# Edge counts of a graph kernel: one routing register a step, and the low one-hots of the late steps made on GpSimd

## The chip, the cores and the metric

The kernel runs on one core of a Trainium2 chip. Its time is the device time in microseconds of one execution. The engines are TensorE (PE for its matmuls, PEld for its weight loads, PEldq or PEq for its sequencer), VectorE (DVE), ScalarE (ACT), GpSimd (POOL) and SyncE (SP), which issues transfers.

## The reference, cut to what matters

A graph of 3125 nodes and 53125 directed edges, sorted by destination, passes through four networks of 128 features (a graph convolution, a two-head attention layer behind a second convolution, a gated network of five layers, an eight-head attention network). The first layer computes

```python
xw = x @ W
deg = jax.ops.segment_sum(ones, dst, num_segments=N)
dinv = jnp.where(deg > 0, jax.lax.rsqrt(deg), 0.0)
norm = dinv[src] * dinv[dst]
msg = xw[src] * norm[:, None]
h = jax.ops.segment_sum(msg, dst, num_segments=N) + b
```

The kernel does most of the sums over edges as dense products. For that it first counts, for each pair of nodes, the edges between them, and keeps the counts as a matrix in DRAM (`adj`). The change lies in that count and in the start of the layer behind it.

## The kernel before, in words

`adjacency_tables` (0 to 36.5 us) reads the edges and prepares, for each of 611 steps, two values for each of 128 edges: `keyt`, which says where among 400 columns the edge counts, and `lowt`, the low seven bits of its source. A step is one tile of 128 edges in one window of 16 destination nodes; there are 196 windows.

`adjacency_counts` runs the steps, each engine through its own list and held to the others by semaphores:

- VectorE makes for step j a one-hot of 400 columns, `count_hot` (line 886, a ring of 8), and every eighth step a block `count_low` (line 876, a ring of 3) with the low one-hots of the next eight steps: 1024 columns, the eight steps interleaved.
- TensorE multiplies the two (line 958, `made`) and adds the product into the PSUM bank of the step's window, one of four. Which bank and which window is data: every fourth step its sequencer loads eight registers from `route_r` (line 923), two a step, moves them (line 924), and before each matmul waits for the step's one-hot (`hots`) and, in an instruction of its own (line 957), for the bank to be free (`freed`, compared with a register).
- ScalarE copies each finished window to `count_stage` (line 975) and clears its bank (line 978). SyncE stores the window to `adj` (line 987).
- Between the steps, by tables of step numbers, TensorE and VectorE also do other work: 20 products that fold two weight matrices of the gated network (lines 938 and 900, from step 40 every 12), five rounds that count the degrees (lines 842 and 846, from step 100), and from step 342 the product x @ W, scaled into `own` (lines 952, 954, 909, 912).
- GpSimd fetches rows for the degrees (line 809), makes `h`, the normalised and rectified x (lines 813 and 816, 70.5 to 94.4 us), stores the folded weights (line 819) and the norms (lines 821 and 823), and casts `own` to the high part of `gcn_parts` (line 827).

After a barrier of all engines `gcn_first` multiplies `gcn_parts`, a high and a low part for each 128 nodes, with the counts. SyncE loads the columns of `adj` in eight groups. VectorE makes the low parts (line 1073), adds the identity to the loaded columns (line 1051, `add_own`) and casts them into `gcn_stream` (line 1061, `widen`); TensorE's matmuls are at line 1138.

## Time and profile before

| | us |
|---|---|
| median of 3 runs | 3405.78 (3403.04 to 3406.25) |
| the profiled execution, its own time | 3405.62 |
| its span, first to last instruction | 3403.8 |
| tables, to the barrier | 36.5 |
| counts, first matmul of a step to the last | 38.3 to 330.5 |
| first matmul of `gcn_first` | 340.3 |

Over the span TensorE is busy 82%, VectorE 52%, ScalarE 40%, GpSimd 28%. These are averages over stages with different limits; for this change only the first 350 us are read. A row of the waits says who waited, and what came last before it could go on; "issue" is time in which an engine's unit had nothing handed to it and no semaphore explains it. Shares of a sequencer are not counted as busy time, so its instructions are read by their durations and by the gaps they leave.

### The profile page before, as it was taken

To read this page: it belongs to the slowest core of one execution; us is meant where nothing else is said; L and a number is where in the kernel's file an instruction comes from. 1 tells how busy PE (TensorE), PEld (TensorE's weight loads), DVE (VectorE), ACT (ScalarE), POOL (GpSimd) and SP (SyncE) were. 2 spreads that over 40 slices of the span, in tenths; PEclk is the share of its full clock that TensorE was granted. 3 is DMA by queue.
4 is the path that set the end of the run, shared out by engine and by line. 5 is a ranking of instruction groups with operands and counts; after the bars stand their busy time and mean duration, and the time that the engine had idled before them with its cause. 6 is when DMAs were issued, how large, how long until landed. Compare 5 with 4: busy or idle time off the path is not lost. (4 is left out here: it accounts for less than half of the span.)

```text
span 3403.8 us, 41036 instructions
## 1 busy us (share of the span) xinstructions
PE 2807.8 (82%) x13998; PEld 2155.1 (63%) x13998; DVE 1760.0 (52%) x4016; ACT 1368.7 (40%) x2596; POOL 961.7 (28%) x779
## 2 busy tenths in 40 slices
PE   5776977899998699999999999999844445446998
PEld 3333875577776578787877787877533334445775
DVE  7987765999977452111122112111534543356994
ACT  3565034699997221111111112111323333342896
POOL 6100043000000453232322231321177777750000
PEclk9977979899999799999999999999855555555999
DMA  4232633101100432121212121310242221113100
GB/s 135 100 101 88 263 130 155 39 40 40 44 1 1 192 150 97 58 92 68 87 63 90 65 92 57 116 70 1 74 141 47 46 46 38 29 21 126 78 35 20
DMA packets 79695, 266.66 MB, mean 78 GB/s; under 512 B 21129, under 2 KB 53344, under 8 KB 70176
## 3 DMA queue, kind: packets, MB, share of 16 engines
q1 hardware_dynamic: 62520, 236.50, 18.6%
q0 software_dynamic: 16976, 27.54, 3.7%
q8 instruction: 121, 1.98, 0.2%
q14 instruction: 78, 0.64, 0.1%
HBM read 232.80 MB, written 31.18 MB: 78 GB/s over the span
## 5 line engine op out<-in xcount | busy, mean ns | idle before, releaser
L2799 PE MATMUL psum<-gate_stream,parts 128*128 128x384 f32 (+1 forms) x3600 | 667.9, 344 | 16.9 <-POOL gate_stream L2872 12.5
L2799 PEld LDWEIGHTS psum<-gate_stream,parts 128*128 128x128 f32 x3600 | 631.5, 189 | 33.8 <-issue 14.4
L2872 POOL CAST gate_stream<-gate_adj 128x1920 fp32r<-128x1920 f16 (+1 forms) x200 | 371.1, 1863 | 851.3 <-PE psum L2799 828.2
L2153 PE MATMUL psum<-gat_h,gat_pair 128*128 128x129 f32 (+1 forms) x3750 | 571.1, 291 | 8.6 <-DVE gat_pair L1957 7.7
L2153 PEld LDWEIGHTS psum<-gat_h,gat_pair 128*128 128x128 f32 (+1 forms) x3750 | 461.5, 191 | 123.4 <-issue 77.7
L1485 POOL DMA_INDIRECT edge_rows<-edge_table,src_idx x440 | 431.7, 981 | 180.7 <-issue 133.7
L2890 DVE SCALAR_TENSOR_TENSOR gate_work<-psum,bhh,gate_work 128x384 f32<-128x384 f32 (+1 forms) x80 | 50.0, 626 | 793.7 <-PE psum L2762 763.1
L1957 DVE SCALAR_TENSOR_TENSOR gat_pair<-gat_above,gat_adj 128x512 f32<-128x512 f32 (+3 forms) x525 | 326.6, 622 | 86.8 <-PE psum L2153 56.7
L2066 ACT ACTIVATE gat_above<-psum,gat_as 128x512 f32<-128x512 f32 (+3 forms) x525 | 329.7, 628 | 41.4 <-PE psum L2141 39.9
L2057 ACT ACTIVATE psum<-gat_ad_rows,gat_as 128x512 f32<-128x512 f32 (+3 forms) x525 | 334.9, 638 | 16.9
L1912 DVE SCALAR_TENSOR_TENSOR gat_acc<-gat_adj,gat_q,gat_acc 128x512 f32<-128x512 f16 (+3 forms) x497 | 328.4, 677 | 0.0
L2816 ACT COPY x<-psum 128x384 f32<-128x384 f32 (+1 forms) x72 | 31.9, 488 | 545.5 <-PE psum L2799 545.5
L1722 PE MATMUL psum<-edge_rows,edge_hot 128*128 128x81 f32 x826 | 179.6, 419 | 86.0 <-DVE edge_rows L1621 86.0
L1722 PEld LDWEIGHTS psum<-edge_rows,edge_hot 128*128 128x128 f32 x826 | 177.2, 332 | 87.6 <-issue 87.2
L958 PE MATMUL psum<-count_hot,count_low 128*128 128x400 f16 x611 | 172.9, 412 | 69.8 <-DVE count_hot L886 47.2
L2141 PE MATMUL psum<-gat_r_rows,gat_pick 6*128 6x512 bf16 (+7 forms) x525 | 189.1, 361 | 0.9 <-ACT gat_r_rows L2075 0.9
L958 PEld LDWEIGHTS psum<-count_hot,count_low 128*128 128x128 f16 x611 | 88.6, 146 | 155.1 <-issue 122.3
L886 DVE TENSOR_SCALAR count_hot<-iota_hot,keyt 128x400 f16<-128x400 f16 x611 | 175.5, 339 | 16.3 <-PE psum L958 13.3
L2844 ACT ACTIVATE gate_work<-psum,brz 128x384 f32<-128x384 f32 (+1 forms) x80 | 47.1, 588 | 331.7 <-PE psum L2775 331.7
L2383 POOL MEMSET parts<- 128x512 f32 x1 | 0.5, 526 | 547.3 <-POOLq L2283 547.3
L975 ACT CAST count_stage<-psum 128x400 f16<-128x400 f32 x196 | 96.8, 494 | 126.2 <-PE psum L958 124.6
L1649 ACT ACTIVATE edge_hot<-iota,edge_minus 128x128 f32<-128x128 f32 x413 | 121.3, 391 | 6.2 <-PEq L2458 6.2
(486 smaller groups left out, 3700.8 us busy)
## 6 DMA issues: line engine op xcount, KB each, us to landing
gate_adj<-adj SPq DMA_DIRECT2D x35, 2400.0 KB, 8.1
gat_adj<-adj SPq DMA_DIRECT2D x8, 3200.0 KB, 11.3
adj<-count_stage SPq DMA_DIRECT2D x196, 100.0 KB, 1.6
gcn_adj<-adj SPq DMA_DIRECT2D x8, 2400.0 KB, 8.2
edge_place<-row_scratch SPq DMA_DIRECT2D x40, 352.0 KB, 3.8
gate_adj<-adj SPq DMA_DIRECT2D x5, 2800.0 KB, 9.1
gcn_adj<-adj SPq DMA_DIRECT2D x4, 3200.0 KB, 10.0
edge_rows<-edge_table,src_idx POOLq DMA_INDIRECT x440
```

The source lines that it names most:

```text
L886: e.tensor_scalar(hot[:, j % HRING, :], iota_hot[:], keyt[:, j:j + 1], None, ALU.is_equal).then_inc(hots, 1)
L958: e.matmul(flat[:, bass.ds(at[j % 4], ROW)], low[:, j // LS % LRING, :, j % LS], hot[:, j % HRING, :], start=False, stop=False, skip_group ...
L1485: e.indirect_dma_start(out=rows[:, c % 2, s, 0:ROWS], out_offset=None, in_=table, in_offset=bass.IndirectOffsetOnAxis(ap=self.src_idx[:, k ...
L1722: mm = e.matmul(flat[:, bass.ds(to[k % 4], SUMS)], hot_of(c)[:, s, :], rows[:, c % 2, s, :], start=False, stop=False, skip_group_check=True)
L1912: e.scalar_tensor_tensor(on, of, q[:, hi, h:h + 1], on, ALU.min, ALU.max).then_inc(most, 1)
L1957: e.scalar_tensor_tensor(on(pair, g % 2), on(above, g % 3), 1e30, cols[:, u % ring, 0:width(u) // W, hi * W:(hi + 1) * W], ALU.min, ALU.mu ...
L2057: e.activation(ps[:, 4 + g % 3, 0:up - lo], ad_rows[:, h, lo:up], ACT.Relu, bias=as8[:, hi, h:h + 1], scale=1.0 - NEG).then_inc(relus, 1)
L2066: e.activation(above[:, g % 3, 0:width(u)], ps[:, 4 + g % 3, 0:width(u)], ACT.Exp, bias=as2[:, hi, h:h + 1]).then_inc(exps, 1)
L2141: e.matmul(ps[:, 4 + g % 3, 0:width(u)], pick[:, h, :], r2_rows[:, u % 2, 0:width(u)], start=False, stop=False, skip_group_check=True).the ...
L2153: mm = e.matmul(ps[0:p, b, a:a + D + 1], pair[:, g % 2, i * P:i * P + p], h1[:, hi, h, :], start=hi == 0 and i % 3 == 0, stop=hi == NT - 1 ...
L2799: mm = e.matmul(ps[:, f, 0:hi - lo], parts[:, t, m, f, :], stream[:, (NGG * i + t // GG) % GR, 0:windows(i), t % GG * W:(t % GG + 1) * W], ...
L2872: e.tensor_copy(stream[:, n % GR, 0:windows(i), :], cols[:, i % 2, 0:windows(i), g * GW:(g + 1) * GW]).then_inc(widened, 1)
```

## The change

1. `route_r` holds one value a step, the window plus 2, instead of two. TensorE's sequencer loads four registers every fourth step and works the bank out of each with a register instruction. The bank of a window moves on by one (lines of ScalarE likewise). The wait for a free bank comes at even steps only, for the bank of the step behind.
2. From step 240 (`LATE` = 30 blocks of 8) VectorE makes no more low one-hots. GpSimd makes them, one comparison of 128 columns a step, from a float32 copy of `lowt` (`lowf`, two more copies on ScalarE in the tables) against the same ring of three blocks, now one step behind the other in it. It starts a block when the steps of the block three before are done, and signals each block (`lower`).
3. GpSimd's other work in the counts is put between its blocks; the low part of `gcn_parts` is now made there too, by a subtraction behind each cast.
4. The first two groups of columns of `adj` are loaded within the counts, and the identity is added to them behind the last steps.
5. Buffers share memory to make room: `near` lies in `gcn_parts`, the weights to be folded in `own`, some tables in `folded`, `h` and `norms`.

```diff
@@ adjacency_tables, vector
-                e.tensor_scalar(win_i[:], win_r[:], 1.0, None, ALU.add).then_inc(made, 1)
+                e.tensor_scalar(route_r[:, 0:BP], win_r[:], 2.0, None, ALU.add).then_inc(made, 1)
...
-                e.tensor_scalar(win_i[:], win_i[:], WR - 1, 9, ALU.bitwise_and, ALU.logical_shift_left).then_inc(made, 1)
-                e.tensor_scalar(route_r[:, 0:BP, 1], win_r[:], 2.0, None, ALU.add)
...
-                e.tensor_copy(route_r[:, 0:BP, 0], win_i[:])
@@ adjacency_tables, scalar
                 e.copy(lowt[:, per * BK:BP], ps[:, 5, 0:BP - per * BK])
+                e.copy(lowf[:, 0:per * BK], ps[:, 4, 0:per * BK])
+                e.copy(lowf[:, per * BK:BP], ps[:, 5, 0:BP - per * BK])
@@ adjacency_counts
+        late = low[:].rearrange("p r q j -> p (r q j)").rearrange("p (r j q) -> p r j q", r=LRING, j=LS)
...
-        near = self.sb("node_near", [P, NT, SE], F32, st)
+        near = parts[:].rearrange("p t m w -> p t (m w)").bitcast(F32)
...
+        own_at = {BSTEPS - 1: (0, 0), BSTEPS - 2: (1, 0), BSTEPS - 3: (1, 1), BSTEPS - 4: (1, 2)}
@@ adjacency_counts, gpsimd
+                def split(n):
+
                     at = slice(group(n)[0], group(n)[-1] + 1)
                     e.wait_ge(hw_taken, n + 2)
-                    e.tensor_copy(parts[:, at, 0, :], own[:, at, :])
+                    e.tensor_copy(parts[:, at, 0, :], own[:, at, :]).then_inc(shaped, 1)
+                    e.wait_ge(shaped, n // 2 + 3)
+                    e.tensor_tensor(parts[:, at, 1, :], own[:, at, :], parts[:, at, 0, :], ALU.subtract)
+
+                for l in range(3):
+                    lay(l)
+                for m in range(LATE, -(-BSTEPS // LS)):
+                    e.wait_ge(made, LS * (m - 2))
+                    for i in range(LS):
+                        inst = e.tensor_scalar(late[:, m % LRING, i, :], self.iota[:], lowf[:, m * LS + i:m * LS + i + 1], None, ALU.is_equal)
+                    inst.then_inc(lower, 1)
+                    if m == 31:
+                        lay(3)
+                    if m == 37:
+                        lay(4)
...
+                    if m >= 48 and m % 4 == 0 and m <= 72:
+                        split((m - 46) // 2)
@@ adjacency_counts, vector
-                    if j % LS == 4 and j + 4 < BSTEPS:
+                    if j % LS == 4 and j // LS + 1 < LATE:
                         lows(j // LS + 1)
...
+                    if j in own_at:
+                        c, i = own_at[j]
+                        t, p = tiles[c][i]
+                        e.wait_ge(loaded[c], 16)
+                        on = cols[:, c, 8 * i:8 * i + p // W, t * W:(t + 1) * W]
+                        e.tensor_tensor(on, on, ident_h[:, 0:p].rearrange("p (w n) -> p w n", n=W), ALU.add)
@@ adjacency_counts, tensor
-                regs = [e.alloc_register(self.name("route_reg")) for _ in range(8)]
...
-                    if j % 4 == 0:
-                        e.load(regs, route[0:1, 2 * j:2 * j + 8])
-                        at = [e.snap(r, min_val=0, max_val=(WR - 1) * 512) for r in regs[0::2]]
-                        need = [e.snap(r, min_val=1, max_val=NW) for r in regs[1::2]]
+                    if j % RL == 0:
+                        regs = [e.alloc_register(self.name("route_reg")) for _ in range(RL)]
+                        e.load(regs, route_r[0:1, j:j + RL])
+                        need = [e.snap(r, donate=True, min_val=1, max_val=NW) for r in regs]
+                        at = [(n & (WR - 1)) * 512 for n in need]
...
+                    if j % LS == 0 and j >= LS * LATE:
+                        e.wait_ge(lower, j // LS - LATE + 1)
                     e.wait_ge(hots, j + 1)
-                    e.wait_ge(freed, need[j % 4])
+                    if j % 2 == 0:
+                        e.wait_ge(freed, need[min(j + 1, BSTEPS - 1) % RL])
@@ adjacency_counts, sync
+                    for c, (lo, hi) in enumerate(spans[:2]):
+                        if w == hi // W + SRING:
+                            for s in range(SRING):
+                                e.wait_ge(stored[s], 16 * (hi // W // SRING))
+                            e.dma_start(cols[:, c, 0:(hi - lo) // W, :], self.adj[:, lo // W:hi // W, :]).then_inc(loaded[c], 16)
@@ gcn_first, vector
-                for n in range(NT // grp):
-                    at = slice(n * grp, (n + 1) * grp)
-                    e.tensor_tensor(parts[:, at, 1, :], own[:, at, :], parts[:, at, 0, :], ALU.subtract).then_inc(far, 1)
...
-                add_own(1)
+                for g in range(NGG):
+                    widen(0, g)
```

TensorE's instructions in the count loop, one group of four steps, before ("ISA" is a register instruction of the sequencer, `freed` and `hots` the waits):

```order
L923 TENSOR_LOAD route_r
L924 ISA
L958 ISA [waits counts_freed,counts_hots]
L958 MATMUL psum<-count_hot,count_low 128x400
L958 ISA [waits counts_freed,counts_hots]
L958 MATMUL psum<-count_hot,count_low 128x400
L958 ISA [waits counts_freed,counts_hots]
L958 MATMUL psum<-count_hot,count_low 128x400
L958 ISA [waits counts_freed,counts_hots]
L958 MATMUL psum<-count_hot,count_low 128x400
```

and now:

```order
L954 TENSOR_LOAD route_r
L992 REGISTER_ALU [waits counts_freed,counts_hots]
L992 ISA
L992 MATMUL psum<-count_hot,count_low 128x400
L992 REGISTER_ALU [waits counts_hots]
L992 ISA
L992 MATMUL psum<-count_hot,count_low 128x400
L992 REGISTER_ALU [waits counts_freed,counts_hots]
L992 ISA
L992 MATMUL psum<-count_hot,count_low 128x400
L992 REGISTER_ALU [waits counts_hots]
L992 ISA
```

The load stands for four registers, the move behind it (line 924) is gone, each step has one register instruction more, and the wait for `freed` stands at every second step.

VectorE around step 240, before (the block of low one-hots, the one-hots, and what is strewn among them):

```order
L876 TENSOR_TENSOR count_low<-iota_low,lowt 128x1024 [waits counts_made]
L886 TENSOR_SCALAR count_hot<-iota_hot,keyt 128x400
L886 TENSOR_SCALAR count_hot<-iota_hot,keyt 128x400 [waits counts_made] x2
L900 COPY folded<-psum 128x384 [waits fold_laid1,fold_made]
L886 TENSOR_SCALAR count_hot<-iota_hot,keyt 128x400 [waits counts_made] x2
L852 MEMSET node_after 128x1 [waits degree_ended]
L853 COPY node_after<-node_until 128x24
L886 TENSOR_SCALAR count_hot<-iota_hot,keyt 128x400 [waits counts_made] x3
L876 TENSOR_TENSOR count_low<-iota_low,lowt 128x1024 [waits counts_made]
L886 TENSOR_SCALAR count_hot<-iota_hot,keyt 128x400
L886 TENSOR_SCALAR count_hot<-iota_hot,keyt 128x400 [waits counts_made] x6
L900 COPY folded<-psum 128x384 [waits fold_laid0,fold_made]
```

and now:

```order
L900 TENSOR_TENSOR count_low<-iota_low,lowt 128x1024 [waits counts_made]
L911 TENSOR_SCALAR count_hot<-iota_hot,keyt 128x400
L911 TENSOR_SCALAR count_hot<-iota_hot,keyt 128x400 [waits counts_made] x2
L931 COPY folded<-psum 128x384 [waits fold_laid1,fold_made]
L911 TENSOR_SCALAR count_hot<-iota_hot,keyt 128x400 [waits counts_made] x2
L876 MEMSET node_after 128x1 [waits degree_ended]
L877 COPY node_after<-node_until 128x24
L911 TENSOR_SCALAR count_hot<-iota_hot,keyt 128x400 [waits counts_made] x10
L931 COPY folded<-psum 128x384 [waits fold_laid0,fold_made]
L911 TENSOR_SCALAR count_hot<-iota_hot,keyt 128x400 [waits counts_made] x12
```

The block at the head of each list is the one of steps 232 to 239; before, the next block (steps 240 to 247) follows after eight one-hots; now there is none behind it.

GpSimd at the same place, before, from the stores of folded rows to the end of the counts:

```order
L819 DMA folded_rows<-folded 128x1536 [waits fold_kept] x5
L821 DMA norm_rows<-norm_t 25x128 [waits first_taken]
L823 DMA norms<-norm_rows 128x3200 [waits first_norm_kept]
L827 CAST gcn_parts<-own 128x4x128 [waits first_taken] x6
L827 CAST gcn_parts<-own 128x128 [waits first_taken]
L805 UNCONDITIONAL_BRANCH [waits fold_laid1,fold_laid0,first_norm_in]
```

and now, from the first comparisons on (the block of steps 240 to 247), and around the first cast of `own`:

```order
L838 TENSOR_SCALAR count_low<-iota,ht_15 128x128 [waits counts_made]
L838 TENSOR_SCALAR count_low<-iota,ht_15 128x128 x7
L838 TENSOR_SCALAR count_low<-iota,ht_15 128x128 [waits counts_made]
L838 TENSOR_SCALAR count_low<-iota,ht_15 128x128 x7
L823 DMA folded_rows<-folded 128x1536 [waits fold_kept]
L838 TENSOR_SCALAR count_low<-iota,ht_15 128x128 [waits counts_made]
```

```order
L849 DMA norms<-norm_rows 128x3200 [waits first_norm_kept]
L838 TENSOR_SCALAR count_low<-iota,ht_15 128x128 [waits counts_made]
L838 TENSOR_SCALAR count_low<-iota,ht_15 128x128 x7
L829 CAST gcn_parts<-own 128x4x128 [waits first_taken]
L831 TENSOR_TENSOR gcn_parts<-own,gcn_parts 128x4x128 [waits first_shaped]
L838 TENSOR_SCALAR count_low<-iota,ht_15 128x128 [waits counts_made]
L838 TENSOR_SCALAR count_low<-iota,ht_15 128x128 x7
```

The comparisons (line 838) stand between all that GpSimd did there, and each cast has a subtraction behind it.

## Rows read from the trace of the kernel before

**Rows 1.** Busy time by stretches, whole core; columns as its first row says

```profile
core 0: us, PE busy (x) PEld busy (x) DVE busy (x) ACT busy (x) POOL busy (x), PEclk, DMA share, GB/s
38.30:153.30 115.00, 82.63 (x289) 44.55 (x289) 103.95 (x285) 60.40 (x140) 50.37 (x54) 0.91 0.35 113
153.30:330.50 177.20, 129.43 (x485) 69.68 (x483) 141.78 (x465) 108.08 (x248) 6.47 (x11) 0.84 0.27 91
```

**Rows 2.** The same two stretches, line 958 alone: busy us, instructions, clock, DMA share, GB/s

```profile
38.30:153.30 115.00, 57.10 (x224) 32.58 (x225) 0.91 0.35 113
153.30:330.50 177.20, 115.32 (x389) 56.00 (x387) 0.84 0.27 91
```

**Rows 3.** TensorE's sequencer, by line: duration ns min/median/max, first and last start

```profile
L923 PEldq TENSOR_LOAD <-route_r x153: 587/592/1162, 37.0 to 328.6; - x153
L924 PEldq FUSED_REGOPS  x153: 80/150/158, 37.8 to 329.3; - x153
L957 PEldq EVENT_SEMAPHORE  x611: 51/51/51, 38.1 to 330.1; - x153
L958 PEldq FUSED_REGOPS  x611: 37/37/47, 38.2 to 330.2; - x153
```

**Rows 4.** Instructions in order of time, weight loads: start us, us, idle before

```profile
226.07 0.58 PEld L958 LDWEIGHTS psum<-count_hot,count_low 128*128 128x128 f16 x3
227.81 0.81 PEld L958 LDWEIGHTS psum<-count_hot,count_low 128*128 128x128 f16 x4 [1.16 <-issue]
```

**Rows 5.** A later stage: the load of four registers, columns as in rows 3

```profile
L1720 PEldq TENSOR_LOAD <-edge_out_r x117: 328/333/338, 2574.0 to 3074.3; - x117
```

**Rows 6.** Who waited for whom, 153.3 to 331 us: us in total, times, longest

```profile
PEld psum L958 <- issue: 81.1, 100, 1.5
```

**Rows 7.** VectorE: two one-hots in order of time, and three lines by duration

```profile
223.53 0.55 DVE L886 TENSOR_SCALAR count_hot<-iota_hot,keyt 128x400 f16<-128x400 f16 x2
...
L876 DVE TENSOR_TENSOR count_low<-iota_low,lowt x77: 628/691/725, 36.9 to 324.9; 128x1024 f16<-128x1024 f16 x77
L846 DVE TENSOR_REDUCE node_until<-node_less x5: 1473/1475/1481, 97.3 to 144.2; 128x5 f32<-128x1280 bf16 x5
L900 DVE COPY folded<-psum x20: 537/548/553, 60.6 to 177.2; 128x384 f32<-128x384 f32 x20
```

**Rows 8.** GpSimd by line and shape: busy us, mean ns, idle before, releaser

```profile
L813 POOL TENSOR_SCALAR h<-x,scale,shift 128x128 f32<-128x128 f32 x25 | 15.4, 625 | 0.1
L816 POOL TENSOR_SCALAR h<-h 128x3200 f32<-128x3200 f32 x1 | 8.4, 8418 | 0.1
L827 POOL CAST gcn_parts<-own 128x512 fp32r<-128x512 f32 x6 | 3.8, 640 | 80.7 <-DVE own L912 80.7
L827 POOL CAST gcn_parts<-own 128x128 fp32r<-128x128 f32 x1 | 0.3, 320 | 13.5 <-DVE own L912 13.5
L1213 POOL CAST gcn_stream<-gcn_adj 128x1920 fp32r<-128x1920 f16 x20 | 35.4, 1809 | 9.7 <-DVE gcn_adj L1226 8.4 <-PE psum L1309 1.3
```

**Rows 9.** GpSimd beside VectorE: line 813, line 886 meanwhile, both in order of time

```profile
L813 POOL TENSOR_SCALAR h<-x,scale,shift x25: 438/518/1761, 70.5 to 85.4; 128x128 f32<-128x128 f32 x25
...
70.50:86.00 15.50, 9.59 (x33) 1.00 0.27 88
...
85.69 8.86 DVE L886 TENSOR_SCALAR count_hot<-iota_hot,keyt 128x400 f16<-128x400 f16 x3
86.01 8.42 POOL L816 TENSOR_SCALAR h<-h 128x3200 f32<-128x3200 f32 x1
```

**Rows 10.** GpSimd by line, 153.3 to 331 us: the stores of folded rows

```profile
L819 POOL DMA_DIRECT2D folded_rows<-folded x2 | 1.2, 611 | 44.1 <-DVE folded L900 44.1
```

**Rows 11.** From one stage to the next in order of time, all engines

```profile
335.06 0.23 DVE L1070 CAST gcn_ident<-ident 128x128 f16<-128x128 f32 x1 [7.41 <-PEq L805]
339.65 1.70 DVE L1061 CAST gcn_stream<-gcn_adj 128x640 fp32r<-128x640 f16 x4
340.29 1.08 PE L1138 MATMUL psum<-gcn_stream,gcn_parts 128*128 128x128 f32 x4 [9.26 <-DVE gcn_stream L1061]
```

120 lines of the change are left out of this document (56 added, 64 removed).

## The prediction

> **What bounds the kernel now.** The change lies in the counting stage and in the start of the stage behind it, so I split the span there. The busy time by stretches [rows 1] gives 115.0 us for steps 0 to 223 (38.3 to 153.3 us) and 177.2 us for steps 224 to 610 (153.3 to 330.5 us). The same stretches for line 958 alone count the steps: 224 matmuls of the first, 389 of the second by the view's edges, 387 by the loop [rows 2]. That is 0.51 and 0.458 us a step. No engine is full in the second stretch: TensorE is busy 129 of 177 us, VectorE 142, ScalarE 108, GpSimd 6. What fills it is TensorE's sequencer. The waits put 81.1 us down to "issue" before the weight loads [rows 6], and the order of time shows the pattern: three or four loads close together, then a hole, with the groups starting 1.74 us apart [rows 4]. Inside a group the loads are 0.22 us apart (0.58 us for three, the last 0.14 long). So 1.74 - 3 x 0.22 = 1.08 us pass between groups, of which the register load takes 0.592 and the instruction that moves its eight values 0.150 [rows 3]. Of the rest 0.22 is the ordinary step and 0.12 are two gaps of 0.06. At 1.74 us for four steps, 387 steps need 168 of the 177 us. VectorE needs 0.23 us for a one-hot of 400 columns (0.55 us for two, the second one 0.32 long) and some 0.6 for a block of low one-hots every eight steps, 0.31 a step [rows 7].
>
> **One register a step.** Four registers are loaded every fourth step, not eight. Line 1720 loads four registers in 0.333 us [rows 5], so the load gives back 0.26. The move is gone, with its gap: 0.15 + 0.06 = 0.21. Added is one register instruction a step, which works out the bank; none of its kind is in the trace. Its nearest neighbours on that queue take 0.037 and 0.051 us [rows 3] with a gap of about 0.055, so 0.09 to 0.11; it takes over the wait for the one-hot. The separate wait for a freed bank (0.051 + 0.055) comes on every second step only, two fewer in a group. Sum: -0.26 - 0.21 + 4 x 0.10 - 2 x 0.106 = -0.28 us; I take -0.26, 1.48 us a group or 0.37 a step. Bounds: at 0.04 each the group is 1.24; at 0.21, as dear as the old move with its gap, 1.92.
>
> Before step 224 that is worth 56 x 0.26 = 14.6 us at most. Not all arrives. From step 100 to 208 VectorE does, every 12 steps, one half of a degree round (1.48 us; the other half is as long) and a fold copy (0.55), so 0.31 + 0.12 + 0.04 = 0.47 us a step [rows 7] against the 0.49 it runs at now: of the 7 us that fall there about 2.5 stay. The one-hot that stands 8.36 us beside a GpSimd instruction (below) stays as it is. I take **-9 us**, between -3 and -13. The wait at an even step is for the bank of the odd one behind it, up to one step early; ScalarE clears banks two windows ahead, so I cost it at nothing, up to 2 us.
>
> **Low one-hots on GpSimd.** VectorE loses 47 blocks of about 0.6 us, which is no gain: it does not bound those steps. GpSimd gets 47 x 8 = 376 comparisons of 128 columns. It starts each block once the block three before it is used up, so the first starts at step 224 for use at 240, and from then on the blocks run as fast as the slower of GpSimd and TensorE. The nearest row is the same operation, shape and per-partition scalars, with two arithmetic operations: line 813, 0.438 us at least and 0.518 in the median [rows 8, 9]. The spread is VectorE's: 33 one-hots ran beside these 25 instructions. Only those beside a two-input VectorE instruction are much longer, and of that kind none but four small ones is left after step 240. With one one-hot a step I take 0.443 us. That is above the 0.37 of the sequencer, so **GpSimd becomes the bound from step 240**: 376 x 0.443 = 166.6 us.
>
> GpSimd also has other work in this stretch, now with TensorE behind it. Two stores of folded rows and two transfers of the norms, 0.6 us each [rows 10], come to 3 us with gaps. The high parts were cast there before (0.640 us, the last 0.320 [rows 8]), under no deadline; now each is followed by a wait and a subtraction of 512 columns that no row shows. The bounds are the cast's 0.64 and 1.35, by the 8418 / 3200 = 2.63 ns a column of line 816; I take 1.2, as it has two inputs. Six such pairs at 1.95 and one at 0.8 make 12.5 us. With 2 us for the start and the last block the stretch is 166.6 + 3 + 12.5 + 2 = 184 against 177.2: **+7 us**. A dearer or cheaper comparison moves this by 3.8 us for each 0.01 us.
>
> **The next stage starts early.** Now VectorE stands idle 7.4 us until the barrier at 335 us, then adds the identity and waits for the first columns; TensorE's first matmul is at 340.29 [rows 11]. The change has loaded and corrected the first two groups of columns by then and made the low parts, so only one cast of 0.42 to 0.49 us stands between the barrier and TensorE: first matmul about 335.9, **-4.4 us**. The barrier still waits for the last stores, as now. The cover is real only if TensorE was last there, and it was: its 50 short matmuls run without a hole once started. The new transfers and four additions of 0.22 us in the count loop cost up to 1 us. In the tables two row operations and a copy less on VectorE stand against two more copies on ScalarE in front of the root that VectorE waits for: nothing, within 1 us.
>
> Sum, from the profiled execution's 3405.62 us, which is the median of the runs shown to within 0.2: 3405.6 - 9 + 7 - 4.4 = **3399 us**.
>
> **Two rules against the rows.** While GpSimd ran line 816, one VectorE one-hot was held for its whole 8.4 us [rows 9]; beside line 813 more one-hots than GpSimd instructions went through, at 0.29 us each. The Trainium skill (SBUF — State Buffer, "Who interferes with whom") says that GpSimd and a VectorE instruction in a two-port mode take a shared port for the whole instruction and that the second one fully blocks. By that rule comparison and one-hot would run one behind the other: the second rival below. The long instruction agrees with it; the short ones do so in part only.
>
> The skill (GPSIMD Engine Reference, "Elementwise — side-by-side cycle accounting") also gives 1.03 cycles an element for bodies of at most two operations, an estimate of some 110 ns for 128 columns beside the fixed cost. The cast rows agree with that slope, line 813 does not. By that rule the first rival below holds.
>
> **Rivals.**
> - *The comparison is as cheap as a cast.* A cast of 128 columns takes 0.320 us and 1920 take 1.809, 0.83 ns a column [rows 8]. At 0.32 GpSimd needs 376 x 0.32 + 17 = 137 us and is hidden; the sequencer bounds all steps: 97 groups x 0.26 = 25 us gained. 3405.6 - 9 - 25 - 4.4 = 3367. Against it: both rows of this very operation are dearer than casts of their size.
> - *One operation is dearer than two* (slower than before). Line 816 has one operation and no arithmetic but a choice, as a comparison has. With a cast's fixed 0.21 us its 8.418 us mean 2.56 ns a column, so 0.54 us for 128, or 0.50 where the next overlaps. 376 x 0.52 + 17.5 = 213 us, +36: 3428 (3421 to 3436). It decides from 0.48 us a comparison on, where the loss of the late steps passes both gains.
> - *GpSimd and VectorE take turns* (slower too). The one-hot held behind line 816 ends 0.12 us after it [rows 9]. If GpSimd then waits for it each time, a step costs 0.44 + 0.12 = 0.56: 376 x 0.56 + 17.5 = 228, +51: 3443. Against it: line 813's median of 0.518 with more than one one-hot beside it.
> - *The registers bring nothing*, the new instruction being as dear as the old move. Then the -9 is lost and +7 stays, since GpSimd bounds the late steps: 3408.
>
> **How the numbers follow.** Forecast (comparison 0.42 to 0.47 us, 3392 to 3410) 0.36; cheap comparison, with the prices between it and 0.42 (3362 to 3391), 0.20; dearer operation 0.23; turns 0.11; no gain from registers 0.10. 0.2% is 6.8 us, about what a measurement of this kernel can tell from no change. Faster by more (under 3399): the cheap case and more than half of the forecast, 0.40. Within it (3399 to 3412): the rest of the forecast and most of the last case, 0.24. Slower: 0.36. The range leaves out the lower half of the cheap case and most of the turns: 3368 to 3438.
>
> **What would show it.** In the profile of the changed kernel: the load of registers at 0.33 us and groups 1.5 us apart before step 240; the register instruction's own duration; GpSimd busy about 95% from step 224, its comparison's median near 0.45 (0.32 or 0.54 for the rivals); TensorE waiting for GpSimd in bursts, one hole every eight steps; one-hots of VectorE at 0.31 to 0.35 us, not 0.45; TensorE's first matmul of the next stage within 1.2 us of the barrier. The prediction is wrong if GpSimd is idle in the late steps, or if its comparison is over 0.48 us.

## The result, and the profile of the changed kernel

The changed kernel takes **3449.8 us** (median of four runs, 3444.5 to 3452.9) where the kernel before takes 3404.4 (median of four, 3401.8 to 3406.3). The ratio is 1.013, with a 95% interval from 1.0115 to 1.015: slower by about 45 us, clear of the noise though under 2%. The forecast was 3399, faster by 0.2%, with a range up to 3438; the time lies above that range.

The profiled execution took 3447.4 us, 41.8 more than that of before. The matmuls of the counting stage give the places. Its first step starts at 37.35 us (38.30 before), step 224 at 143.3 (153.3) and step 610 at 386.4 (330.5). Busy time by stretches, the changed kernel, columns as in rows 1:

```profile
37.35:143.30 105.95, 84.92 (x289) 43.59 (x288) 103.06 (x285) 60.72 (x140) 49.16 (x54) 0.95 0.47 153
143.30:386.45 243.15, 153.18 (x485) 60.63 (x482) 142.19 (x422) 109.11 (x248) 241.21 (x394) 0.66 0.20 66
```

Rows 1 had 115.0 and 177.2 us in these two places. The first stretch gained the 9 us that were forecast. The second one took 66 us more, where 7 were forecast, and GpSimd is busy for 241.2 of its 243.2 us. Who waited for whom in it (us in total, times, longest), where rows 6 had 81.1 us of "issue" and nothing of GpSimd:

```profile
PEld psum L992 <- issue: 158.3, 184, 3.9
...
DVE count_hot L911 <- PE psum L992: 97.1, 70, 3.1
PE psum L992 <- POOL count_low L838: 81.3, 46, 3.2
```

TensorE waited 46 times for a block of low one-hots, 81.3 us in all, up to 3.2 us at once; there are 47 blocks. VectorE in turn waited 97.1 us for TensorE to use up its one-hots. So GpSimd sets the pace. What it did in that stretch, by line and shape (busy us, mean ns, idle before), which answers to rows 8 and 10:

```profile
L838 POOL TENSOR_SCALAR count_low<-iota,ht 128x128 f16<-128x128 f32 x376 | 227.5, 621 | 19.2 <-PE psum L992 19.0
L831 POOL TENSOR_TENSOR gcn_parts<-own,gcn_parts 128x512 fp32r<-128x512 f32 x6 | 7.6, 1265 | 0.5
L829 POOL CAST gcn_parts<-own 128x512 fp32r<-128x512 f32 x6 | 3.6, 604 | 0.0
```

And line 838, a step's comparison, by duration (min/median/max ns):

```profile
L838 POOL TENSOR_SCALAR count_low<-iota,ht x376: 590/613/840, 143.6 to 385.0; 128x128 f16<-128x128 f32 x188
```

A comparison takes 613 ns in the median and never less than 590. Its 227.5 us are 0.605 us for each of the 376; the forecast had 0.443. The subtraction of 512 columns takes 1265 ns (1.2 was taken) and the cast 604 (0.64).

The registers, in the sequencer's rows (rows 3 and 5 were their measure):

```profile
L954 PEldq TENSOR_LOAD <-route_r x153: 327/332/888, 36.0 to 383.5; - x153
...
L992 PEldq ALU_OP  x611: 32/32/42, 36.9 to 386.2; - x153
L992 PEldq FUSED_REGOPS  x611: 46/46/46, 37.0 to 386.3; - x153
```

The load of four takes 332 ns in the median (rows 5: 333), the new register instruction, ALU_OP, 32 ns, and the old move is gone. The next stage's start, all engines in order of time, which answers to rows 11:

```profile
386.36 0.10 PEld L992 LDWEIGHTS psum<-count_hot,count_low 128*128 128x128 f16 x1 [0.25 <-issue]
...
389.81 1.29 DVE L1095 CAST gcn_stream<-gcn_adj 128x640 fp32r<-128x640 f16 x3 [6.14 <-PEq L808]
...
390.36 0.90 PE L1161 MATMUL psum<-gcn_stream,gcn_parts 128*128 128x128 f32 x3 [3.38 <-DVE gcn_stream L1095]
```

TensorE's first matmul starts 0.55 us after VectorE's first cast behind the barrier, and 3.9 us after the last step's; before it was 340.29 - 330.49 = 9.8.

Up to the first matmul of the next stage the account is -1.0 (tables), -9.1, +66.0, -5.9: together +50.1 us. The rest, -8.3, comes in stages whose code is the same. Most of it (-5.7) falls behind the edge stage, a late stage that gathers rows by edge. From its last matmul to the last one of the program it is 3386.6 - 3079.7 = 306.9 us in the kernel before and 301.2 here. The matmuls' first and last start, in the changed kernel:

```profile
L1745 PE MATMUL psum<-edge_rows,edge_hot_end x54: 342/417/422, 3116.0 to 3127.2; 128*128 128x81 f32 x54
...
L2176 PE MATMUL psum<-gat_h,gat_pair x3750: 273/275/583, 661.1 to 3428.4; 128*128 128x129 f32 x190, 128*64 128x129 f32 x8
```

Nine further profiles below, of kernels with the changed kernel's code there, gave 306.5 to 307.0 us, and the one with the registers alone 310, so this is no effect of the change; against the medians of the runs, a few us of any such account are the profiled execution's own.

### The profile page after: what moved, and what is told of

Its sections match the earlier page's. It is cut to its first block and busy times, and to the rows that moved or that the text cites. A ratio compares the mean times of both kernels' runs of the same rounds, so it can differ in the third digit from the quotient of the medians.

```text
span 3445.8 us, 41526 instructions
## 1 busy us (share of the span) xinstructions
PE 2826.5 (82%) x13998; PEld 2139.8 (62%) x13998; DVE 1752.9 (51%) x3962; ACT 1370.3 (40%) x2598; POOL 1190.9 (35%) x1162
## 5 line engine op out<-in xcount | busy, mean ns | idle before, releaser
L992 PE MATMUL psum<-count_hot,count_low 128*128 128x400 f16 x611 | 197.1, 439 | 109.7 <-POOL count_low L838 81.3
L911 DVE TENSOR_SCALAR count_hot<-iota_hot,keyt 128x400 f16<-128x400 f16 x611 | 200.9, 379 | 99.2 <-PE psum L992 98.2
L838 POOL TENSOR_SCALAR count_low<-iota,ht 128x128 f16<-128x128 f32 x376 | 227.5, 621 | 19.2 <-PE psum L992 19.0
L1745 PEld LDWEIGHTS psum<-edge_rows,edge_hot 128*128 128x128 f32 x826 | 177.2, 332 | 87.4 <-issue 87.0
L992 PEld LDWEIGHTS psum<-count_hot,count_low 128*128 128x128 f16 x611 | 73.2, 120 | 232.4 <-issue 202.7
```

The source lines that it names most:

```text
L838: inst = e.tensor_scalar(late[:, m % LRING, i, :], self.iota[:], lowf[:, m * LS + i:m * LS + i + 1], None, ALU.is_equal)
L911: e.tensor_scalar(hot[:, j % HRING, :], iota_hot[:], keyt[:, j:j + 1], None, ALU.is_equal).then_inc(hots, 1)
L992: e.matmul(flat[:, bass.ds(at[j % RL], ROW)], (low[:, j // LS % LRING, :, j % LS] if j < LS * LATE else late[:, j // LS % LRING, j % LS, : ...
L1745: mm = e.matmul(flat[:, bass.ds(to[k % 4], SUMS)], hot_of(c)[:, s, :], rows[:, c % 2, s, :], start=False, stop=False, skip_group_check=True)
```

## The experiments

The theory after the result: the late stretch lasts 376 times the price of GpSimd's comparison, and some 15 us of its other work; that price was mis-sized by 0.16 us, and all else in the prediction stands. The rivals: what is queued beside the comparisons is the cost; GpSimd and VectorE hold each other up; a GpSimd that makes the operand costs something besides its price.

**All low one-hots on VectorE again.** Everything else of the change stays:

```diff
+ON_POOL = ()
-                    for i in range(LS):
-                        inst = e.tensor_scalar(late[:, m % LRING, i, :], self.iota[:], lowf[...], None, ALU.is_equal)
-                    inst.then_inc(lower, 1)
+                    if m in ON_POOL:
+                        ...
-                    if j % LS == 4 and j // LS + 1 < LATE:
+                    if j % LS == 4 and j + 4 < BSTEPS and j // LS + 1 not in ON_POOL:
                         lows(j // LS + 1)
```

> The changed kernel with one part undone: VectorE makes the low one-hots of every step, 8 steps at a time, and GpSimd keeps its casts, subtractions and transfers at their places. If the time of the changed kernel was lost in GpSimd's 376 comparisons (376 x (0.60 - 0.443) us = 59 us above the forecast), this kernel drops nearly all of the +66 us of the stretch of steps 224 to 610 and keeps the registers' gain there: about 177 - 387/4 x 0.26 = 152 us instead of 243, so about 3450 - 91 = 3359 us (3350 to 3372). If the loss lay in what is queued beside them (the splits, or the moved transfers), the stretch stays above 190 us and the time near 3400 or over. If one register a step gives nothing in the late steps, the stretch is 177 us and the time 3384.

Measured: 3361.3 us, ratio 0.9873 (0.9856 to 0.9889). It was run a second time beside two further kernels (below): 3360.3 us, 0.9871 (0.9855 to 0.9888). The second run's stretch of steps 224 to 610, and TensorE's weight loads there in order of time (start us, us, idle before):

```profile
143.86:294.86 151.00, 120.14 (x484) 66.00 (x482) 141.27 (x469) 107.76 (x248) 15.54 (x18) 0.99 0.32 106
```

```profile
229.35 0.36 PEld L994 LDWEIGHTS psum<-count_hot,count_low 128*128 128x128 f16 x2 [0.71 <-issue]
...
230.90 0.43 PEld L994 LDWEIGHTS psum<-count_hot,count_low 128*128 128x128 f16 x2 [0.66 <-issue]
...
232.44 0.40 PEld L994 LDWEIGHTS psum<-count_hot,count_low 128*128 128x128 f16 x2 [0.57 <-issue]
```

151.0 us instead of 243.2, with GpSimd's casts, subtractions and transfers still in their places: the first rival falls. The groups of four start 1.54 to 1.55 us apart (229.35, 230.90, 232.44), where rows 4 had 1.74. The granted clock is 0.99 here, 0.84 in the kernel before and 0.66 in the changed one, means between the two levels of 1.2 and 2.4 GHz, lowest where TensorE idled longest. In the changed kernel the low clock cost nothing, since TensorE waited for GpSimd anyway. How much of the 26 us gained here is the clock's can be read from the kernel before, which ran at either level in its late steps. Its counting matmuls alone, in a stretch at the low level and in one at the high level, columns as in rows 2:

```profile
180.00:203.70 23.70, 19.74 (x52) 7.45 (x51) 0.50 0.28 94
204.00:220.80 16.80, 9.94 (x38) 5.29 (x38) 1.00 0.51 173
```

At the low level its groups of four with no other matmul among them start 1.82 us apart as a mean (17 groups; 52 steps in 23.7 us give the same). At the high level it is 1.76 (49 groups; the second row also holds products for x @ W). Such groups at the high level in the kernel of this experiment have 1.51 (74 groups). The low level filled 58 of the 177 us, some 32 groups, so the clock's share of the gain is about 2 us and the shorter queue's the rest.

**The registers alone, in the kernel before.** The edit is the change's own: four registers, the bank worked out from each, one wait for two steps. Low one-hots, buffers and the next stage's start stay as before.

```diff
-                    if j % 4 == 0:
-                        e.load(regs, route[0:1, 2 * j:2 * j + 8])
+                    if j % RL == 0:
+                        e.load(regs, route_r[0:1, j:j + RL])
...
+                        at = [(n & (WR - 1)) * 512 for n in need]
...
-                    e.wait_ge(freed, need[j % 4])
+                    if j % 2 == 0:
+                        e.wait_ge(freed, need[min(j + 1, BSTEPS - 1) % RL])
```

> The kernel before with the register routing alone (4 registers for 4 steps, one wait for two steps, the ring of windows turned by one); low one-hots on VectorE, everything else as before. Theory, that the early stretch's -9 us and the late steps' -0.26 us for each 4 steps are the registers': 115.0 - 9 = 106 us in the early stretch, 177.2 - 25 = 152 us in the late one, together 3405 - 34 = 3371 us (3365 to 3380). Rival, that VectorE's work is next in the late stretch and takes most of it back (VectorE is busy there for 0.74 of the stretch): 3390 to 3396 us. Rival, that the registers bring nothing: 3404.

Measured: 3367.8 us, ratio 0.9888 (0.9872 to 0.9905). Its two stretches:

```profile
37.08:142.98 105.90, 84.67 (x289) 43.31 (x288) 103.28 (x285) 60.91 (x140) 54.96 (x53) 0.95 0.38 122
...
142.98:293.45 150.47, 120.59 (x484) 65.92 (x482) 136.36 (x465) 107.70 (x248) 6.45 (x11) 0.99 0.32 107
```

The registers alone bring 9.1 and 26.7 us. The kernel above is 6.5 us faster still. At least 4.6 of these have a place in the traces: there TensorE's next stage starts 3.8 us after the last step (295.33 to 299.11), here 8.4 (293.44 to 301.85), because VectorE waits 3.3 us for the columns behind the barrier. So the early start of the next stage is worth about 4.6 us, as forecast (4.4).

**What makes the comparison dear.** First in place: a multiplication and an addition with two scalars' addresses instead of the comparison.

```diff
-                        inst = e.tensor_scalar(late[...], self.iota[:], lowf[...], None, ALU.is_equal)
+                        inst = e.tensor_scalar(late[...], self.iota[:], zero[:, 0:1], zero[:, 1:2], ALU.mult, ALU.add)
```

> The changed kernel with each of GpSimd's 376 comparisons replaced by a multiplication and an addition with two scalars that are zero, same input, same output tile and type: the low one-hots of the late steps are zero, so the edge counts of these steps are left out and the output is not the reference's. Theory A, that the comparison itself is dear on GpSimd and plain arithmetic is not: one takes 0.44 us as in line 813 of the kernel before, the late stretch falls to about 185 us and the time to about 3392 us. Theory B, that the dear part is what both share (reading a scalar's address, an output of 2 bytes, the walk over 128 columns beside a busy VectorE): 0.58 to 0.61 us again and 3445 to 3455 us.

Measured: 3402.1 us, ratio 0.9994 (0.9984 to 1.0005), stretch 194.3 us:

```profile
L839 POOL TENSOR_SCALAR count_low<-iota,count_zero 128x128 f16<-128x128 f32 x376 | 178.7, 487 | 19.2 <-PE psum L994 19.0
```

```profile
143.87:338.13 194.26, 139.93 (x485) 55.42 (x482) 134.66 (x422) 108.58 (x248) 192.31 (x394) 0.75 0.25 83
```

Theory A's direction, but not its size: this form takes 0.487 us as a mean in place (178.7 / 376 = 0.475 from one to the next), not 0.44. It is the form of line 813, from which the prediction took its price. Even had the comparison cost as much as that form, the kernel would only have been level with the one before.

Then GpSimd alone, and VectorE's one-hots with and without it, in a small program:

```python
for i in range(R):
    e.tensor_scalar(oh[:, 0, i, :], iota[:], one(i), None, ALU.is_equal)                # line 54
...
for i in range(R):
    e.tensor_scalar(of[:, 1, i, :], iota[:], one(i), one(i), ALU.mult, ALU.add)         # line 60
for i in range(R):
    e.tensor_scalar(of[:, 2, i, :], iota[:], one(i), None, ALU.mult)                    # line 64
```

> All of the reference's computation is left out; GpSimd alone does 8 each of tensor_scalar over 128x128: comparison with a scalar's address, to 2-byte and to 4-byte output; comparison with a constant; multiplication and addition with addresses, to 4 and to 2 bytes; multiplication alone; maximum with a constant; comparison from 2-byte input; comparison greater-or-equal; a copy; then 2048 columns of maximum, 2048 of multiplication and addition, 1024 of comparison, 1024 of subtraction of two tiles. Then 24 hot comparisons of 400 columns on VectorE: alone, beside 12 comparisons of GpSimd, beside 12 multiply-adds. Theory A (the comparison is dear): 0.58 us for the three comparisons to 2 bytes and about 0.44 for multiply-add. Theory B (output of 2 bytes is dear): 0.58 for every 2-byte output, 0.44 for 4 bytes. Theory C (only beside VectorE is it dear): below 0.48 us for all of them here, and above 0.55 only in the last two parts. If VectorE's hot is held up by GpSimd, its mean goes from 0.30 alone to 0.38 or more beside GpSimd.

By line and shape (busy us, mean ns, idle before):

```profile
L93 POOL TENSOR_SCALAR beside<-iota,ptr 128x128 f16<-128x128 f32 x12 | 7.3, 627 | 6.3 <-ACTq L84 6.3
L88 DVE TENSOR_SCALAR hot<-cols,ptr 128x400 f16<-128x400 f16 x24 | 7.2, 375 | 0.3 <-PEq L79 0.3
L98 DVE TENSOR_SCALAR hot<-cols,ptr 128x400 f16<-128x400 f16 x24 | 6.2, 333 | 0.6 <-DVEq L84 0.6
L103 POOL TENSOR_SCALAR beside_f<-iota,ptr 128x128 f32<-128x128 f32 x12 | 6.0, 512 | 0.4 <-POOLq L84 0.4
L83 DVE TENSOR_SCALAR hot<-cols,ptr 128x400 f16<-128x400 f16 x24 | 5.7, 318 | 66.8 <-PEq L49 66.8
L73 POOL TENSOR_SCALAR wide<-wide_in 128x2048 f32<-128x2048 f32 x1 | 5.4, 5359 | 0.0
L64 POOL TENSOR_SCALAR of<-iota,ptr 128x128 f32<-128x128 f32 x8 | 4.7, 601 | 0.0
...
L54 POOL TENSOR_SCALAR oh<-iota,ptr 128x128 f16<-128x128 f32 x8 | 4.6, 600 | 12.3 <-PEq L49 12.3
L56 POOL TENSOR_SCALAR of<-iota,ptr 128x128 f32<-128x128 f32 x8 | 4.6, 600 | 0.0
L58 POOL TENSOR_SCALAR oh<-iota 128x128 f16<-128x128 f32 x8 | 4.0, 527 | 0.0
L66 POOL TENSOR_SCALAR of<-iota 128x128 f32<-128x128 f32 x8 | 4.0, 524 | 0.0
L60 POOL TENSOR_SCALAR of<-iota,ptr 128x128 f32<-128x128 f32 x8 | 3.4, 446 | 0.0
...
L75 POOL TENSOR_SCALAR wide_h<-wide_in,ptr 128x1024 f16<-128x1024 f32 x1 | 2.8, 2846 | 0.0
...
L74 POOL TENSOR_SCALAR wide<-wide_in,ptr 128x2048 f32<-128x2048 f32 x1 | 2.0, 2042 | 0.0
```

Line 54 is the comparison as the change has it: 600 ns with nothing beside it. It is not the comparison as such: a multiplication alone (line 64) costs 601. It is not the output's type: 4 bytes (line 56) cost the same 600. A constant in place of the scalar's address saves 73 ns (line 58, 527; the maximum, line 66, 524). The width tells the rest. One operation: (2846 - 600) / 896 = 2.51 ns a column for the comparison and (5359 - 524) / 1920 = 2.52 for the maximum. Multiplication with addition: (2042 - 446) / 1920 = 0.83 ns, the slope of a cast (rows 8). So the comparison of 128 columns is 128 x 2.51 = 0.321 and 0.279 us of fixed time. All three theories as I had put them fall: the first blamed the comparison, the second the 2-byte output, the third VectorE.

VectorE's part is small. Beside one-hots the comparison takes 627 instead of 600 ns (line 93), the multiplication with addition 512 instead of 446 (line 103), and the one-hots 375 and 333 instead of 318 (lines 88, 98, 83). If they took turns, 24 one-hots (5.7 us alone, line 83) and 12 comparisons (7.3 us, line 93) would need 13.0 us; line 88's 24 had 7.2 busy us and only 0.3 idle. It is larger where VectorE also makes blocks of low one-hots, with two input tiles: in the kernel below that gives GpSimd every second block, a comparison takes 670 ns as a mean, 771 for the 43 of 192 that ran beside such a VectorE instruction, and 640 for the others.

**More forms.** The question was whether a second operation makes any body cheap.

```python
e.tensor_scalar(oh[:, 1, i, :], iota[:], one(i), 1.0, ALU.is_equal, ALU.mult)           # line 55
e.tensor_scalar(oh[:, 3, i, :], iota[:], 1.0, 0.0, ALU.mult, ALU.add)                   # line 59
e.tensor_scalar(oh[:, 5, i, :], iota[:], one(i), one(i), ALU.mult, ALU.mult)            # line 63
e.tensor_scalar(oh[:, 6, i, :], iota[:], one(i), one(i), ALU.add, ALU.add)              # line 65
e.tensor_scalar(oh[:, 9, i, :], iota[:], one(i), None, ALU.add)                         # line 71
```

> All of the reference's computation is left out; GpSimd alone, 8 each over 128x128 to 2-byte output: comparison and then multiplication by a scalar's address; by the constant 1; comparison and addition of 0; multiplication and addition with constants; subtraction and multiplication; two multiplications; two additions; multiplication and comparison; multiplication and maximum; addition alone; a subtraction and a multiplication of two tiles; and 256, 512 and 2048 columns of comparison, of multiplication with addition, and of comparison with multiplication. The first such run gave 600 ns for every form of one operation (comparison or multiplication alike) and 446 ns for multiplication with addition. Theory S (what is dear is a tensor_scalar with only one operation): every form of two operations 440 to 460 ns, addition alone 600, and a comparison with a second operation saves 0.15 us a step. Theory F (multiplication with addition is the one cheap form): all other pairs 600 ns or more, by 128 columns, and about 2.5 ns for a further column against 0.83.

```profile
L80 POOL TENSOR_SCALAR wide_h<-wide_in,ptr 128x2048 f16<-128x2048 f32 x1 | 7.3, 7311 | 0.0
...
L65 POOL TENSOR_SCALAR oh<-iota,ptr 128x128 f16<-128x128 f32 x8 | 6.3, 835 | 0.0
...
L55 POOL TENSOR_SCALAR oh<-iota,ptr 128x128 f16<-128x128 f32 x8 | 5.6, 729 | 0.0
L78 POOL TENSOR_SCALAR wide_h<-wide_in,ptr 128x2048 f16<-128x2048 f32 x1 | 5.5, 5502 | 0.0
L71 POOL TENSOR_SCALAR oh<-iota,ptr 128x128 f16<-128x128 f32 x8 | 4.7, 668 | 0.0
L63 POOL TENSOR_SCALAR oh<-iota,ptr 128x128 f16<-128x128 f32 x8 | 3.5, 483 | 0.0
...
L59 POOL TENSOR_SCALAR oh<-iota 128x128 f16<-128x128 f32 x8 | 2.2, 320 | 0.0
L77 POOL TENSOR_SCALAR wide_h<-wide_in,ptr 128x512 f16<-128x512 f32 x1 | 2.1, 2146 | 0.0
...
L75 POOL TENSOR_SCALAR wide_h<-wide_in,ptr 128x512 f16<-128x512 f32 x1 | 1.6, 1628 | 0.0
```

This program stood on another chip, and its forms with a scalar's address take some 60 to 85 ns longer than in the first program: the comparison of 2048 columns 5502 ns, where 600 and 1920 columns at 2.51 give 5419. (Line 71, one addition, took 668, but no single comparison of 128 columns was in this program.) The chip is not shown to be the reason. In the kernel with every second block on GpSimd the comparison took 671 ns as a mean on this chip and 670 on another. The expectations below that speak of a slower chip rest on this reading. The slope is the same: (5502 - 1628) / 1536 = 2.52 ns a column for the comparison, between 512 and 2048 columns, and (7311 - 2146) / 1536 = 3.36 for the comparison with a second operation. Two additions cost 835 ns, a comparison with a multiplication 729. Two multiplications cost 483 and a multiplication with addition of constants 320. So theory F holds with one correction: the cheap pairs are multiplication with addition and two multiplications. No comparison was among the cheap forms.

**A dearer comparison, in place.** The same output by a second operation:

```diff
-                        inst = e.tensor_scalar(late[...], self.iota[:], lowf[...], None, ALU.is_equal)
+                        inst = e.tensor_scalar(late[...], self.iota[:], lowf[...], 1.0, ALU.is_equal, ALU.mult)
```

> The changed kernel with a second operation in each of GpSimd's comparisons (a multiplication by the constant 1), the output unchanged. Alone, on the slower chip, this form took 738 ns where a single operation took 668, and each further column 3.4 ns against 2.5: so 0.66 to 0.68 us here, beside VectorE about 0.69. Theory: stretch = 376 x 0.69 + 15 = 274 us (268 to 280) and 3450 + 31 = 3481 us (3472 to 3490). Rival, that the second operation makes it the cheap form (0.45 to 0.49): stretch 194 us and 3402 us.

```profile
L838 POOL TENSOR_SCALAR count_low<-iota,ht 128x128 f16<-128x128 f32 x376 | 264.3, 719 | 19.2 <-PE psum L992 19.1
```

```profile
168.97:448.89 279.92, 157.25 (x485) 61.67 (x482) 151.34 (x422) 109.31 (x248) 277.98 (x394) 0.63 0.17 58
```

The stretch is 279.9 us, at the upper end of what the theory gave (274, 268 to 280): the price was 264.3 / 376 = 0.703 us, where 0.69 was taken. The rival of a cheap form falls. Only the ratio can be set against other runs, since this chip ran the kernel before in 3722 us: 1.0194 (1.0176 to 1.0213), against 1.022 expected.

**The old registers, with GpSimd's comparisons.** The change's register routing undone:

```diff
-                        e.load(regs, route_r[0:1, j:j + RL])
+                        e.load(regs, route_r[:].rearrange("p j n -> p (j n)")[0:1, 2 * j:2 * j + 8])
...
-                    if j % 2 == 0:
-                        e.wait_ge(freed, need[min(j + 1, BSTEPS - 1) % RL])
+                    e.wait_ge(freed, need[j % 4])
```

> The changed kernel with its register routing undone (8 registers for 4 steps, a wait at each step), GpSimd's comparisons kept from step 240. Theory, that from there GpSimd's price times 376 sets the pace and TensorE's queue only waits: the stretch of steps 224 to 610 stays at 243 us (240 to 247), the early one goes back from 106.0 to 115 us, and the time is 3450 + 9 = 3459 us. Rival, that both parts add up along the whole stage: 243 + 25 us in the late stretch and 3484.

```profile
172.98:419.22 246.24, 154.18 (x485) 62.43 (x483) 143.71 (x422) 109.13 (x248) 244.40 (x394) 0.63 0.20 66
```

246.2 us: eight registers or four, the late stretch is the same, since TensorE's queue has time while GpSimd works. The rival of two costs that add up falls. The ratio, on the same chip as the last one, is 1.0213 (1.0195 to 1.0231), more than the 1.016 expected, and more than the last one's, although its late stretch is 34 us shorter. The excess lies in the edge stage, whose code is the same: its matmuls span 688 us here (2786.2 to 3474.5) and 645 in the last one (2815.8 to 3461.3). So the ratios of these two kernels bear no finer reading, and the stretches are what counts. The early steps can't be read there: they took 134.1 us with the old registers, but 131.4 (the kernel above) and 127.0 (one below) with the new ones where the kernel before takes about 3720 us.

**A cheaper operation, in place.** A multiplication and an addition of constants:

```diff
-                        inst = e.tensor_scalar(late[...], self.iota[:], lowf[...], None, ALU.is_equal)
+                        inst = e.tensor_scalar(late[...], self.iota[:], 0.0, 0.0, ALU.mult, ALU.add)
```

> The changed kernel with each of GpSimd's 376 comparisons replaced by a multiplication by the constant 0 and an addition of the constant 0: the low one-hots of the late steps are zero, the edge counts of these steps are left out, and the output is not the reference's. This form took 0.32 us alone (on the slower chip), against 0.60 for the comparison. With 0.605 us a step the stretch of steps 224 to 610 took 243 us, with 0.487 it took 194 us: 376 times the price, and 14 to 16 us of other work. At 0.30 us this sum is 128 us and below TensorE's and VectorE's own pace; so by the theory the stretch stops at 145 to 152 us and the time is 3350 to 3360 us. Rival, that GpSimd in this place costs something besides its price (hand-over of tiles for each block, late transfers): 160 us or more and 3370 us or over.

```profile
L838 POOL TENSOR_SCALAR count_low<-iota 128x128 f16<-128x128 f32 x376 | 103.5, 304 | 48.1 <-PE psum L992 48.0
```

```profile
143.17:295.65 152.48, 115.72 (x485) 48.69 (x482) 129.75 (x422) 107.72 (x248) 117.86 (x394) 1.00 0.32 105
```

```profile
PEld psum L992 <- issue: 79.6, 186, 1.1
```

3361.3 us (0.9872, 0.9852 to 0.9892), stretch 152.5: GpSimd is busy for 118 of it and no longer the bound, and the time is that of all low one-hots on VectorE, no better. The rival of a cost besides the price falls. No engine is full (VectorE 130 us, TensorE 116); the weight loads wait 79.6 us for "issue", as they did in rows 6: the bound is in the main again what it was in the kernel before (the matmuls waited another 24.4 us for VectorE's one-hots). The time was expected at 3350 to 3360, the stretch at 145 to 152, so both came out just above. The prices in place and the stretches together, sorted by price:

| GpSimd's operation | its busy us | stretch 224 to 610 | difference |
|---|---|---|---|
| mult, add, constants | 103.5 | 152.5 | 49.0 |
| mult, add, addresses | 178.7 | 194.3 | 15.6 |
| comparison (the change) | 227.5 | 243.2 | 15.7 |
| comparison, old registers | 230.7 | 246.2 | 15.5 |
| comparison and mult | 264.3 | 279.9 | 15.6 |

In four of five kernels the stretch is GpSimd's operation time and the same 15.5 to 15.7 us. In the fifth that sum would be 119, and something else stands at 152.

**A part of the blocks on GpSimd.** If TensorE's queue bounds the rest, GpSimd may take some blocks for nothing, and gain nothing:

```diff
+ON_POOL = tuple(range(30, 77, 2))
```

> The changed kernel with GpSimd making the low one-hots of every second block of 8 steps (24 of the 47 blocks from step 240), VectorE those of the others. Theory, that the price of one comparison times their number is what the change costs: two blocks of steps take 16 x 0.39 = 6.2 us, of which GpSimd needs 8 x 0.61 = 4.9, so it is not late except around its subtractions; VectorE, busy for 0.94 of this stretch where it makes all of them, has 24 x 0.69 = 16 us less to do. The stretch of steps 224 to 610 takes 145 to 152 us, the time is 3355 to 3363 us (3361 where VectorE makes all). Rival, that GpSimd's comparisons slow VectorE's hots (0.32 to 0.375 us beside them) and so the whole: stretch 160 us and 3370. Rival, that anything of GpSimd in the order costs through hand-overs of tiles: over 3380.

This run stood on the chip of 3715 us for the kernel before: 3669.5, ratio 0.9877 (0.9839 to 0.9915), stretch 153.7 us. So it was run again, with every third block beside it:

> Every second block of 8 from step 240 on GpSimd, once more. Its first run stood on a chip on which the kernel before took 3715 us, and its ratio there was 0.9877, as that of all on VectorE. Theory that TensorE's own pace (about 0.38 us a step) bounds both: equal to it within 0.2%, stretch 148 to 153 us. Rival, that what VectorE has less to do (24 x 0.69 = 16 us, busy for 141 of 151 us) comes through in full: stretch 140 us or less, 10 us below it.

> Every third block of 8 from step 240 on GpSimd (16 of 47), the others on VectorE: same theory as for every second block, within 0.2% of all on VectorE; GpSimd's 128 comparisons are then 78 us of a stretch of some 150.

> The changed kernel with the low one-hots of every step on VectorE, once more, beside the two divisions below on one chip: ratio 0.987 as in its first run, stretch of steps 224 to 610 151 us.

Measured on one chip: 3360.3 us with all on VectorE, 3362.1 with every second block on GpSimd (0.9875, 0.9859 to 0.9892), 3365.3 with every third (0.9881, 0.9864 to 0.9897). The late stretch of every second and of every third block:

```profile
143.50:296.57 153.07, 118.94 (x485) 57.49 (x482) 145.71 (x445) 107.68 (x248) 140.86 (x210) 0.99 0.32 105
```

```profile
143.81:296.48 152.67, 119.77 (x485) 60.18 (x482) 144.22 (x453) 107.73 (x248) 100.05 (x146) 0.98 0.32 105
```

No division gains. VectorE has fewer blocks to make and yet is busy for 145.7 us instead of 141.3, since its one-hots take longer beside GpSimd (372 ns as a mean of all instead of 346). With every third block GpSimd is busy for only 100 us of the stretch, and the stretch differs by only 0.4 us. The kernel of this study with the lowest time, by less than the noise over these, is the one that has all of the change but GpSimd's comparisons.

## Why the prediction was wrong

- **What bounds the kernel:** right. The sequencer's work sets the late steps; with less of it the groups without other matmuls went from 1.77 to 1.51 us in the median.
- **Registers:** right. The load (0.333 taken, 0.332 measured), the move (gone) and the waits are as put down. The register instruction takes 0.032 us and its gap. Taken were 1.48 us a group and 0.26 gained; measured, 1.51 and 0.26, as the median of the 77 late groups without other matmuls (the starts shown above are three of the longer ones). Early steps -9 taken, -9.1 measured. Where nothing else bounds, the late steps gain 26 to 27 us (25 by the cheap rival's sum).
- **The price of a comparison on GpSimd:** this is the term that failed. Taken: 0.443 us, by line 813 as "the same operation, shape and per-partition scalars, with two arithmetic operations" [rows 8, 9]. Measured: 0.605. That row's own form cost 0.475 when put in this place, between its least (0.438) and its median (0.518) in rows 9; so 376 x 0.032 = 12 us of the error are the low reading of the row, and 376 x 0.130 = 49 us are one comparison taken to be no dearer than two arithmetic operations. Together 376 x 0.162 = 61 us, less 2 for other work that was cheaper than taken, are the 59 by which the stretch passed its forecast of 184. The reading "GpSimd becomes the bound from step 240" was right.
- **The choice of the row.** Two operations don't bound one from above here. The same rows held the better neighbour: line 816, one operation, 8418 ns for 3200 columns [rows 8], 2.6 ns a column where casts had 0.83. The rival *one operation is dearer than two* used it, and was right in its mechanism: 2.56 ns a column against 2.51 measured. Its size fell short because it took a cast's fixed 0.21 us (measured 0.20 with a constant, 0.28 with a scalar's address) and up to 0.04 us off for overlap (measured 0.621 as a mean, 0.605 busy: 0.016). With 0.28 and 0.016 it would have read 0.59 us, and about 240 us for the stretch. Its own threshold (slower from 0.48 us) holds: the multiply-add kernel at 0.475 to 0.487 came out level with the one before.
- **GpSimd's other work in the stretch:** 12.5 + 3 + 2 = 17.5 us taken, 15.6 measured.
- **The next stage's start:** -4.4 taken, -5.9 in the trace of the change, 4.6 between two kernels with and without it.
- **The rival of turns** gives nearly the right price (0.56), by a mechanism that isn't there: the comparison costs 600 ns with VectorE idle, and VectorE's one-hots cost it 27 ns.
- **The range** ended at 3438, just above the 0.54 us of the dearer operation. That operation was not in the trace, and the range took one reading of its fixed part for the dearest there could be; a fixed part only 0.07 us larger put the time outside.

On the two rules that were weighed: the Trainium skill (GPSIMD Engine Reference, "Elementwise — side-by-side cycle accounting") gives one slope, 1.03 cycles an element, for bodies of at most two operations. The runs agree for multiplication with addition (0.83 ns a column, where the prediction's estimate by that page, 110 ns for 128 columns, means 0.86) and for casts, not for a comparison or a maximum alone (2.5 ns) nor for a comparison with a second one. The Trainium skill (SBUF — State Buffer, "Who interferes with whom") has the later of two instructions on the shared port wait for the whole of the first. Beside 128-column comparisons of GpSimd the one-hots were slowed from 318 to 375 ns and not blocked for the instruction's length; whether they used that port at all no run here shows.

## What to carry to other kernels

Before work moves to another engine, price that engine's instruction by a row of the same number and kind of operations, and split the row into a fixed part and a slope by two widths; if no row of that kind is there, let the worst neighbour set the range. And ask first what bounds the steps once the work has gone: here even a GpSimd at half the price brought nothing, since the queue of TensorE, not VectorE, was the bound, so the move could only lose. An edit that shortens the bound itself (registers) was worth 36 us, and was hidden behind the other one.

## What the runs showed of the hardware

- GpSimd's tensor_scalar has several slopes: 0.83 ns a column for multiplication with addition, 2.5 ns for a comparison or a maximum alone, and 3.36 ns for a comparison with a multiplication. A multiplication by itself (601 ns for 128 columns) costs as much as a comparison, and more than a multiplication with an addition (446).
- A scalar read by its address costs the comparison 73 ns more than a constant.
- One kernel, two chips: every second block on GpSimd took 3362 us on one and 3669 on another. Most of the difference is in the edge stage, whose rows come by indirect transfers; its matmuls, on the one chip and on the other:

```profile
L1747 PE MATMUL psum<-edge_rows,edge_hot x826: 275/417/503, 2533.5 to 3020.3; 128*128 128x81 f32 x166
```

```profile
L1747 PE MATMUL psum<-edge_rows,edge_hot x826: 275/417/503, 2688.8 to 3330.8; 128*128 128x81 f32 x166
```

They span 487 us (2533.5 to 3020.3) and 642 us (2688.8 to 3330.8), each matmul 417 ns in the median on both. That is 155 us of the 305 between the two profiles. Another 132 pass in the same stage ahead of the first of these matmuls (from the first one of line 1765, at 2434.3 and at 2457.3 us), and 21 in the early steps of the count. On that chip the early steps of the count took 127.0 us instead of 105.9 with the same instructions. What is different about it the runs don't show.
